# A seven-bank ring of TensorE results laid out as three pairs and a single bank, with the softmax normalisation moved to GpSimd

## The chip, the cores and the metric

The kernel runs on one core of one Trainium2 chip. The metric is the device time of one execution in microseconds, and less is better. Times of an execution are read from the trace of one profiled execution.

## The reference, cut to what matters

The input x is 8 images of 256 channels by 1024 pixels (32x32). Four blocks follow each other:

```python
# L0: single-head self-attention with 32 latent channels over the 1024 pixels, then attention over 128 concepts
# L1: a 10-class map, its norms, a small gated MLP, added back to x
# L2: group norm, then 8-head attention, 32 channels per head, over 1024 x 1024 pixels
qkv = einsum('oc,bct->bot', w_qkv, group_norm(x)) + b_qkv
weight = softmax(einsum('bct,bcs->bts', q * scale, k * scale), axis=-1)
a = einsum('bts,bcs->bct', weight, v)
x = x + (einsum('oc,bct->bot', w_proj, a) + b_proj)
# L3: group norm, then for every pixel an attention of its 8 heads with each other, projected and added to x
```

## The kernel before

Everything is float32. The attention of L0 and L2 is done in "windows". A window `u` is one unit: four heads (L2: half the heads of one image, so two windows an image, `par` 0 and 1) or four images of L0's one head. There are 2 windows of L0 and 16 of L2, 18 in all, each of `STEPS` = 16 steps. A window has two halves of eight steps. A half holds 512 queries, and each of its steps takes 128 keys.

All five engines run through the same list of steps, each with its own instruction order, written out by `window_jobs`. In step s TensorE does, in this order:

- `scores(u, par, s)`, L626 to L638: the scores of four heads, 128 keys by 512 queries each, as four rounds of four matmuls (32 contraction rows a head; HI and LO are a split of the float32 values, and the last round adds the negated maximum). Each head has a PSUM bank of its own.
- `values(u, par, s - 1)`, L652: eight matmul instructions that add exp(scores) x V of the step before into the bank AV. In text, V.
- the jobs of the step, `jobs[s]`. The one in nearly every step is `max`, L603: four matmuls of the scores in the other orientation (128 queries by 512 keys), whose row maxima VectorE takes for a coming half (`row_max`, L1292). The eight of a half stand in its first seven steps, two of them in step 1. Others are `qk` (L688; VectorE splits it at L1267 and L1268), `v` (L678), `post` (the output projection, L705), `sums` (L662 and L667, the softmax sums over the keys; step 1 of each half), `flip` (turns the maxima, last step of each half) and `spread` (L712, step 6 of each half).

ScalarE takes exp of each head's bank (L1034) into the buffer PR, which holds four steps. GpSimd adds the exps of the steps of a half (L1201, twelve adds a half, two a step), beginning once the `sums` of the half before are done (`half_done`), and it may lag some steps behind. In one window of each image GpSimd also makes the next image's normalised input (`norm_apply`, L1172 to L1181).

Every result that TensorE leaves in PSUM for another engine takes the next bank of a ring of seven; the eighth bank is AV. TensorE may write a bank once its last reader has released it. When it wants a bank that isn't free it waits, and so does all that is behind it, since its instructions stay in order. The helpers at issue:

```python
def fill(reader, tally, back):          # TensorE
    slot = ring.place()
    if slot in held:
        wait(pe, *held[slot])
    held[slot] = (reader, tally.now() - back)
    return RING[slot]
```

At the end of a half its unnormalised output must leave AV, and its sums are inverted:

- ScalarE copies AV to OHU after the exps of the next half's step 0 (`keep_values`, L1000). It first waits for `norm_done`, which says that the outputs of the half before that are normalised. The first V of the next half, which TensorE issues in its step 1, waits for this copy (`half_kept`).
- ScalarE copies the sums to RC (`keep_sums`, L1006), and a DMA spreads them over R16. VectorE inverts R16 (`invert`, step 3). A DMA brings the inverses back to RC (`return_inverse`, step 4). TensorE's `spread` multiplies them by a block matrix, which repeats the row of each head over its 32 rows of PSUM (step 6), and VectorE multiplies OHU by it (`normalise`, L1317) and raises `norm_done`.

After the windows comes L3, with other code. It takes about the last quarter of the time.

Of the kernel before, what the change touches and what calls it, by code (L numbers as in the profile page):

```python
# [15 lines left out]

# [9 lines left out]
D = 32  # L26
# [3 lines left out]
EXPS = H * STEPS  # L30
SLOTS = 7
# [5 lines left out]
RETURN_AT = 4  # L37
SPREAD_AT = 6
# [28 lines left out]
class Ring:  # L67


    def __init__(self):  # L70
        self.at, self.slots = 0, tuple(range(SLOTS))

    def place(self):
        self.at += 1
        return self.slots[(self.at - 1) % len(self.slots)]
# [4 lines left out]
    def align(self, to=0):  # L80
        while self.at % SLOTS != to:
            self.at += 1

    def only(self, slot):
        self.at, self.slots = 0, (slot,)


def places(job, single):

    if job[0] == "v":  # L90
        return 2 if single else 1
    return {"max": 4, "stats": 0, "negate": 0, "reread": 0, "concepts": 4, "softmax": 0, "turn": 4,
            "classes": 2, "norms": 2, "pool": 0, "regate": 0, "write": 4}.get(job[0], 1)
# [9 lines left out]
QK_ORDER = ((1, 0), (1, 1), (0, 0), (0, 1))  # L103


def maxima(half):

    return [("max", half, t, keys) for t in range(TILES_HALF) for keys in range(2)]


def window_jobs(post=False, nxt=True, gn=False, ahead=0, trail=True, single=False):
# [5 lines left out]
    for half in range(2):  # L117
# [5 lines left out]
        if half == 1 or trail:  # L123
            jobs[first + SUM_AT].insert(1, ("sums",))
            jobs[first + SPREAD_AT].append(("spread", half - 1))
    if nxt:
        for step, job in zip((1, 2, 3, MT + (3 if post or gn or single else 7)), QK_ORDER):
            jobs[step].append(("qk",) + job)
        parts = (6, MT + 1) if single else (7, MT + 1, MT + 1, MT + 2) if gn else (4, 6, 7, MT + 2)
        for n, step in enumerate(parts):  # L130
            jobs[step].append(("v", n))
    if post:
        for step, job in zip((4, 6, MT + 4, MT + 7), ((0, 0), (1, 0), (0, 1), (1, 1))):
            jobs[step].append(("post",) + job)
    if ahead:
# [3 lines left out]
        jobs[first + 2].append(("gn", 0, ahead))  # L139
    if gn:  # L140
        jobs[MT + 4].append(("gn", 1, 1))
# [29 lines left out]
def first_jobs():  # L171
# [6 lines left out]
            ("norms",): [("v", n) for n in range(4)]}  # L178
# [8 lines left out]
def program(nc, x, w_l0, w_o, w_o_t, concepts, concepts_t, gammas, conv_w, conv_wt, conv_b, lin1_t, lin2_t,  # L187
# [8 lines left out]
    with ctx:  # L196
# [19 lines left out]
        RC = sb("RC", [P, HALF])  # L216

# [116 lines left out]
        RING = [S4[:, n, :] for n in range(4)] + [RB[:, 0, :], RB[:, 1, :], SUM[:, :]]  # L334
        RING_SUM, RING_LAST = 6, 5
# [21 lines left out]
        stage_ready = sem("stage_ready")  # L357
# [10 lines left out]
        inverse_in = sem("inverse_in")  # L368
        norm_done = sem("norm_done")
# [1396 lines left out]
```

## Time and profile before

| | |
|---|---|
| median of 3 runs | 1921.55 us (1916.68 to 1927.38) |
| the profiled execution | 1920.26 us, of which the span of the trace is 1918.5 us |
| busy share of the span | PE (TensorE matmul) 89%, DVE (VectorE) 72%, POOL (GpSimd) 71%, ACT (ScalarE) 41%, PEld (TensorE weight load) 40% |

The busy time of PE is modelled: matmuls overlap each other in the array, and each is drawn with its whole latency. So a stretch with PE at 99% can still hold time in which TensorE issues nothing. That is better seen in the starts of its instructions.

### The profile page before, as it was taken

How to read it: one execution, taken by the hardware profiler on the slowest of the kernel's cores; microseconds unless marked ns; L12 is line 12 of the kernel's file. 1: busy time of each engine (PE TensorE's matmuls, PEld its weight loads, DVE VectorE, ACT ScalarE, POOL GpSimd, SP SyncE). 2: the span in 40 equal slices, each digit the busy share in tenths (PEclk: the TensorE clock that was granted, in tenths of full speed). 3: DMA queues.
4: the chain of work that ended last, by engine and by line, in shares of the span. 5: the costliest groups of instructions: out<-in, count | busy, mean ns of one | idle time of the engine just before them, and what ended most of it. 6: DMA issues, size and time to landing. Idle time of an engine off the chain costs nothing.

```text
span 1918.5 us, 37187 instructions
## 1 busy us (share of the span) xinstructions
PE 1702.5 (89%) x15160; PEld 773.6 (40%) x15160; DVE 1374.5 (72%) x2153; ACT 787.1 (41%) x1546; POOL 1357.7 (71%) x581
## 2 busy tenths in 40 slices
PE   5897765799999999999999999999997678889974
PEld 2332222344344444344344344444442345555541
DVE  5677567887777877767867877777771158878875
ACT  0352401155455555455455455455555233333320
POOL 0573600088788887887888878878789059989996
PEclk8898887799999999999999999999998889999986
DMA  5000030220001001001001010010010211222211
GB/s 189 1 2 1 2 129 0 84 77 23 2 2 67 2 2 67 2 9 60 2 24 45 2 59 11 1 67 2 2 45 1 89 29 55 88 77 75 74 51 47
DMA packets 48432, 75.11 MB, mean 39 GB/s; under 512 B 30804, under 2 KB 31110, under 8 KB 48262
## 3 DMA queue, kind: packets, MB, share of 16 engines
q1 hardware_dynamic: 38758, 72.15, 10.6%
q8 instruction: 120, 1.97, 0.4%
q10 hardware_dynamic: 9504, 0.59, 0.3%
q14 instruction: 50, 0.41, 0.1%
HBM read 44.87 MB, written 25.17 MB: 37 GB/s over the span
## 4 chain that ended last, share of the span: by engine, by line
PE 77%; DVE 13%; issue 3%; ACT 2%; DMA 2%; POOL 1%; SPq 1%; POOLq 0%; DVEq 0%; ACTq 0%
PE AV L652 14%; DVE MX L1292 7%; PE S L626 6%; PE RB L895 6%; PE S L688 4%; PE S L603 3%; PE AV L908 3%; PE RB L626 3%; PE RB L944 3%; PE S L638 2%; PE RB L603 2%; PE S L630 2%; PE S L678 2%; PE RB L688 2%; PE S L634 2%
## 5 line engine op out<-in xcount | busy, mean ns | idle before, releaser
L1201 POOL TENSOR_TENSOR ACC<-ACC,PR 128x1024 f32<-128x1024 f32 x360 | 840.9, 2373 | 34.4 <-ACT PR L1034 34.4
L1034 ACT ACTIVATE PR<-S 128x512 f32<-128x512 f32 x667 | 358.6, 603 | 373.1 <-PE S L638 242.9
L1292 DVE TENSOR_REDUCE MX<-S 128x1 f32<-128x512 f32 x646 | 409.4, 681 | 124.2 <-PE RB L603 60.5
L1201 POOL TENSOR_TENSOR ACC<-PR 128x1024 f32<-128x1024 f32 x72 | 168.9, 2368 | 343.0 <-ACT PR L1034 131.6
L652 PE MATMUL AV<-PR,VT 128*32 128x512 f32 x2304 | 312.9, 616 | 3.8 <-ACT PR L1034 3.3
L1292 DVE TENSOR_REDUCE MX<-RB 128x1 f32<-128x512 f32 x336 | 218.5, 681 | 73.8 <-PE S L603 57.0
L1034 ACT ACTIVATE PR<-RB 128x512 f32<-128x512 f32 x328 | 183.7, 604 | 168.9 <-PE S L638 63.4
L626 PE MATMUL S<-HI 32*128 32x512 f32 x667 | 195.6, 493 | 6.2 <-DVE NMR L1305 2.5
L1227 POOL TENSOR_TENSOR PR<-WO,WRK 128x1792 f32<-128x1792 f32 x32 | 155.6, 4883 | 27.9 <-DMA WO<-WO 12.9
L1227 POOL TENSOR_TENSOR PR<-WO,VT 128x1792 f32<-128x1792 f32 x32 | 155.0, 4867 | 10.3 <-DMA WO<-WO 8.3
L603 PE MATMUL S<-HI 32*128 32x512 f32 x646 | 156.2, 507 | 3.4 <-ACT PR L1034 2.8
L1651 DVE TENSOR_REDUCE ENC<-PR 128x256 f32<-128x2048 f32 x64 | 145.9, 2280 | 15.7 <-issue 7.4
L630 PE MATMUL S<-LO,HI 32*128 32x512 f32 x667 | 143.1, 431 | 0.0
L1292 DVE TENSOR_REDUCE MX<-SUM 128x1 f32<-128x512 f32 x170 | 115.8, 681 | 34.4 <-PE S L603 33.7
L638 PE MATMUL S<-NMR,ONER 32*128 32x512 f32 x667 | 131.6, 397 | 0.0
L634 PE MATMUL S<-HI,LO 32*128 32x512 f32 x667 | 131.2, 397 | 0.0
L1034 ACT ACTIVATE PR<-SUM 128x512 f32<-128x512 f32 x157 | 94.8, 604 | 75.3 <-PE S L638 69.1
L626 PEld LDWEIGHTS S<-HI 32*128 32x128 f32 x667 | 78.7, 183 | 108.9 <-ACT PR L1034 39.2
L626 PE MATMUL RB<-HI 32*128 32x512 f32 x328 | 118.1, 491 | 4.0 <-ACT PR L1034 2.0
L603 PE MATMUL RB<-HI 32*128 32x512 f32 x336 | 111.5, 509 | 11.1 <-DVE MX L1292 11.1
L895 PE MATMUL RB<-X 128*32 128x256 f32 x1792 | 111.7, 390 | 10.6 <-ACT X L1099 4.2
L603 PEld LDWEIGHTS S<-HI 32*128 32x128 f32 x646 | 59.4, 186 | 140.3 <-DVE MX L1292 48.7
(357 smaller groups left out, 3250.9 us busy)
## 6 DMA issues: line engine op xcount, KB each, us to landing
X<-out_y SPq DMA_DIRECT2D x24, 1024.0 KB, 5.0
out_y<-X SPq DMA_DIRECT2D x16, 1024.0 KB, 4.9
X<-in_x SPq DMA_DIRECT2D x8, 1024.0 KB, 8.5
OHU<-out_y SPq DMA_DIRECT2D x8, 512.0 KB, 4.4
X<-out_y SPq DMA_DIRECT2D x8, 512.0 KB, 4.1
out_y<-X SPq DMA_DIRECT2D x8, 512.0 KB, 3.1
out_y<-OHU SPq DMA_DIRECT2D x8, 512.0 KB, 3.1
WO<-WO SPq DMA_DIRECT2D x128, 16.0 KB, 1.9
```

Of the source, the lines that this page charges most:

```text
L603: mm(bank(), HI[par][D * h:D * h + D, 0, first:first + P], HI[par][D * h:D * h + D, 1, HALF * keys:HALF * keys + HALF], start=True, stop=T ...
L626: mm(dst[h], HI[par][row, 1, keys], HI[par][row, 0, cols], start=True, stop=False, skip_group_check=True)
L630: mm(dst[h], HI[par][row, 1, keys], LO[par][row, 0, cols], start=False, stop=False, skip_group_check=True)
L634: mm(dst[h], LO[par][row, 1, keys], HI[par][row, 0, cols], start=False, stop=False, skip_group_check=True)
L638: mm(dst[h], ONER[row, :], NMR[row, half, :], start=False, stop=True, skip_group_check=True).then_inc(st_full, 1)
L652: last = mm(AV[D * h:D * h + D, :], VT[par][:, mt, D * h:D * h + D], exps(s, h // 2)[:, HALF * (h % 2):HALF * (h % 2) + HALF], start=(mt = ...
L895: last = mm(dst[D * j:D * j + D, QUARTER * (h % 2):QUARTER * (h % 2) + QUARTER], W3[:, t, C * which + D * h:C * which + D * h + D], xn3(b) ...
L1034: nc.scalar.activation(exps(s, pair)[:, HALF * one:HALF * one + HALF], RING[ring.place()], ACT.Exp, scale=1.0 if i is None else float(D) * ...
L1201: nc.gpsimd.tensor_tensor(ACC[:, pair, :], so_far, exps(s, pair), ALU.add).then_inc(pool_used, 1)
L1227: nc.gpsimd.tensor_tensor(PV[n % 2].rearrange("p (h d g) -> p h d g", h=NHEAD, d=D)[:, heads], PTK[:, st, heads, j, :].unsqueeze(2).broadc ...
L1292: nc.vector.tensor_reduce(out=MX[:, h, t, keys:keys + 1], in_=bank(), op=ALU.max, axis=AX.X).then_inc(ring_free, 1)
L1651: nc.vector.tensor_reduce(out=O3[n % 2], in_=PV[n % 2].rearrange("p (c g) -> p c g", g=NHEAD), op=ALU.add, axis=AX.X).then_inc(o_ready3, 1)
```

## The change

It does four things.

1. The ring is made of three pairs of banks (`PAIR`, `SLOTS` = 3) in place of seven banks. The four heads' scores take two pairs, and so does a `max`. A pair has one release for both its banks. ScalarE takes exp of a pair in one instruction of 128x1024 in place of two of 128x512, and `row_max` reduces a pair in one instruction. The seventh bank, SUM, is a single one (`Single`) outside the ring. `qk`, `v`, `post`, `gn` and `sums` all use it, one after the other.
2. `spread` on TensorE and `normalise` on VectorE go, in L2's windows, and become `settle`: in step 5 of a half ScalarE issues a DMA that repeats the inverses over the rows (`repeat_inverse`, 128 rows of 512 into the new buffer INV), and GpSimd multiplies OHU by it (128x512) after its adds of step 6. GpSimd's multiply raises `norm_done`. There are 31 of these; L0's and the last half keep `spread`.
3. `v` is done four key tiles at a time: two jobs of 16 matmuls a window in place of four of 8.
4. Jobs move. `qk` goes from steps 1, 2, 3 and 11 or 15 to steps 0, 2, 8 and 10, and the order of its four parts changes. `v` goes to steps 4 and 7 or 3 and 7; `post` goes from 4, 6, 12, 15 to 3, 5, 12, 15; `gn` 1 goes from step 12 to 11 (13 in the first image). The `max` tiles go over the first 512 keys and then the second. The semaphore `stage_ready` is dropped for a wait on `ring_free`.

```diff
-SLOTS = 7
+SLOTS = 3
+REPEAT_AT = 5
...
-            jobs[first + SPREAD_AT].append(("spread", half - 1))
+            jobs[first + SPREAD_AT].append(("settle" if settle else "spread", half - 1))
     if nxt:
-        for step, job in zip((1, 2, 3, MT + (3 if post or gn or single else 7)), QK_ORDER):
+        for step, job in zip((1, 2, 3, MT + 3) if single else (0, 2, MT, MT + 2), QK_ORDER):
             jobs[step].append(("qk",) + job)
-        parts = (6, MT + 1) if single else (7, MT + 1, MT + 1, MT + 2) if gn else (4, 6, 7, MT + 2)
-        for n, step in enumerate(parts):
+        for n, step in enumerate((6, MT + 1) if single else (4, 7) if gn else (3, 7)):
             jobs[step].append(("v", n))
...
-        RING = [S4[:, n, :] for n in range(4)] + [RB[:, 0, :], RB[:, 1, :], SUM[:, :]]
-        RING_SUM, RING_LAST = 6, 5
+        PAIR = [S4[:, 0:2, :], S4[:, 2:4, :], RB[:, 0:2, :]]
+        SINGLE = (SUM[:, :], RB[:, 1, :])
...
+            def pair(reader, count):
 
                 slot = ring.place()
                 if slot in held:
                     wait(pe, *held[slot])
-                held[slot] = (reader, tally.now() - back)
-                return RING[slot]
+                held[slot] = (reader, count)
+                return PAIR[slot]
+
+            def single(reader, count):
+
+                if "single" in held:
+                    wait(pe, *held["single"])
+                held["single"] = (reader, count)
+                return spot.bank()
...
                 for h in range(H):
                     row = slice(D * h, D * h + D)
-                    exped.add()
-                    dst.append(fill(exp_done, exped, 0))
+                    if h % 2 == 0:
+                        two = pair(exp_done, exped.add())
+                    dst.append(two[:, h % 2, :])
...
+            def repeat_inverse(n):
+
+                wait(act, inverse_in, 16 * (n + 1))
+                act.dma_start(INV[:, :],
+                              RC[0:P:D, :].unsqueeze(1).broadcast_to([H, D, HALF])).then_inc(repeat_in, 16)
...
-                        nc.scalar.activation(exps(s, pair)[:, HALF * one:HALF * one + HALF],
-                                             RING[ring.place()], ACT.Exp,
+                        nc.scalar.activation(exps(s, pair),
+                                             PAIR[ring.place()].rearrange("p a q -> p (a q)"), ACT.Exp,
...
+                    if jobs and ("settle", half - 1) in jobs[s]:
+
+                        own, n = par if half else 1 - par, 2 * u + half - 1
+                        wait(pool, repeat_in, 16 * (n - 3))
+                        nc.gpsimd.tensor_tensor(OH[own][1 - half], OH[own][1 - half], INV[:, :],
+                                                ALU.mult).then_inc(norm_done, 1)
...
             def row_max(half, t, keys):
-                for h in range(H):
-                    nc.vector.tensor_reduce(out=MX[:, h, t, keys:keys + 1], in_=bank(), op=ALU.max,
-                                            axis=AX.X).then_inc(ring_free, 1)
+                for pair in range(2):
+                    wait(dve, ring_full, drained.add())
+                    nc.vector.tensor_reduce(out=MX[:, 2 * pair:2 * pair + 2, t, keys], in_=PAIR[ring.place()],
+                                            op=ALU.max, axis=AX.X).then_inc(ring_free, 1)
```

## Rows read from the trace of the kernel before

**Rows 1.** The page: busy time by engine, and the chain's shares.

```profile
PE 1702.5 (89%) x15160; PEld 773.6 (40%) x15160; DVE 1374.5 (72%) x2153; ACT 787.1 (41%) x1546; POOL 1357.7 (71%) x581
...
PE 77%; DVE 13%; issue 3%; ACT 2%; DMA 2%; POOL 1%; SPq 1%; POOLq 0%; DVEq 0%; ACTq 0%
```

**Rows 2.** Timeline of PE in one image: start us, length us, V.

```profile
1005.55 1.07 PE L652 MATMUL AV<-PR,VT 128*32 128x512 f32 x8
...
1016.93 1.06 PE L652 MATMUL AV<-PR,VT 128*32 128x512 f32 x8
...
1021.41 1.06 PE L652 MATMUL AV<-PR,VT 128*32 128x512 f32 x8
...
1040.52 1.06 PE L652 MATMUL AV<-PR,VT 128*32 128x512 f32 x8
...
1046.30 1.06 PE L652 MATMUL AV<-PR,VT 128*32 128x512 f32 x8
```

**Rows 3.** Timeline of all engines in step 0 of a window.

```profile
1002.17 1.06 PE L652 MATMUL AV<-PR,VT 128*32 128x512 f32 x8
1002.27 2.06 ACT L1034 ACTIVATE PR<-S 128x512 f32<-128x512 f32 x4 [2.34 <-PE S L638]
...
1003.16 0.50 PE L603 MATMUL RB<-HI 32*128 32x512 f32 x2
...
1003.70 1.29 DVE L1292 TENSOR_REDUCE MX<-RB 128x1 f32<-128x512 f32 x2 [1.81 <-PE S L603]
...
1004.20 0.63 ACT L1000 ACTIVATE OHU<-AV 128x512 f32<-128x512 f32 x1
...
1004.44 0.49 PE L626 MATMUL RB<-HI 32*128 32x512 f32 x1
```

**Rows 4.** Groups by line on DVE: count, busy us, mean ns of one.

```profile
L1292 DVE TENSOR_REDUCE MX<-S 128x1 f32<-128x512 f32 x646 | 409.4, 681 | 124.2 <-PE RB L603 60.5 <-PE S L603 42.0 <-PE SUM L603 19.9
...
L1610 DVE TENSOR_REDUCE SUM<-S 128x256 f32<-128x2048 f32 x16 | 36.7, 2296 | 0.9 <-PE S L923 0.6
L1268 DVE SCALAR_TENSOR_TENSOR LO<-S,X,HI 128x512 fp32r<-128x512 f32 x36 | 27.0, 751 | 1.3
...
L1317 DVE TENSOR_TENSOR OHU<-OHU,S 128x512 f32<-128x512 f32 x22 | 14.9, 676 | 15.0 <-PE S L712 15.0
```

**Rows 5.** Chain that ended last, in order of time: its jobs on TensorE.

```profile
960.00 1.06 PE S L712 x2
...
974.31 1.09 PE S L678 x8
...
1007.06 1.00 PE S L662 x8
1008.05 0.86 PE S L667 x8
...
1018.43 1.92 PE RB L688 x4
```

**Rows 6.** Timeline of POOL over the two windows of one image.

```profile
938.25 4.70 POOL L1201 TENSOR_TENSOR ACC<-PR 128x1024 f32<-128x1024 f32 x2 [7.01 <-PE S L667]
...
974.05 4.69 POOL L1201 TENSOR_TENSOR ACC<-PR 128x1024 f32<-128x1024 f32 x2 [7.85 <-PE RB L667]
...
996.62 9.39 POOL L1201 TENSOR_TENSOR ACC<-ACC,PR 128x1024 f32<-128x1024 f32 x4
1009.38 4.69 POOL L1201 TENSOR_TENSOR ACC<-PR 128x1024 f32<-128x1024 f32 x2 [3.37 <-PE S L667]
1014.03 23.32 POOL L1201 TENSOR_TENSOR ACC<-ACC,PR 128x1024 f32<-128x1024 f32 x10
1044.06 4.70 POOL L1201 TENSOR_TENSOR ACC<-PR 128x1024 f32<-128x1024 f32 x2 [6.71 <-PE RB L667]
...
1077.50 4.69 POOL L1201 TENSOR_TENSOR ACC<-PR 128x1024 f32<-128x1024 f32 x2 [5.45 <-PE RB L667]
```

**Rows 7.** DMA issues: size, median us from issue to landing.

```profile
OHU<-out_y SPq DMA_DIRECT2D x8, 512.0 KB, 4.4
```

More of the change, by code:

```diff
@@ L70, in __init__, with align, bank, last @@
     def __init__(self):
-        self.at, self.slots = 0, tuple(range(SLOTS))
+        self.at = 0
     def place(self):
         self.at += 1
-        return self.slots[(self.at - 1) % len(self.slots)]
+        return (self.at - 1) % SLOTS
     def skip(self, n):
         self.at += n
-    def align(self, to=0):
-        while self.at % SLOTS != to:
+    def align(self):
+        while self.at % SLOTS:
             self.at += 1
[L84 to L93, printed above, removed]
+class Single:
+    def __init__(self, banks):
+        self.n, self.banks = 0, banks
+    def bank(self):
+        return self.banks[self.n]
+    def last(self):
+        self.n = 1
+def places(job):
+    return {"max": 2, "flip": 1, "settle": 0, "concepts": 2, "turn": 2, "classes": 1, "norms": 1, "write": 2}.get(job[0], 0)
 def wait(eng, sem, value):
@@ L690, in qk_product @@
                 last.then_inc(ring_full, 1)
+                kept_qk[u, which, half] = drained.now()
             def group_sums(k, batch):
@@ L818, in after @@
                         pe.wait_ge(pe_ready, pe_need.add())
-                    dst = [bank() for _ in range(H)]
+                    dst = banks() + banks()
                     for j in range(H):
@@ L1050, in window @@
                         return_inverse(2 * u)
+                    for half in range(2):
+                        if s == MT * half + REPEAT_AT and ("settle", half - 1) in jobs[MT * half + SPREAD_AT]:
+                            repeat_inverse(2 * u + half - 1)
                     if early:
@@ L1253, in link, with bank, banks, split_qk @@
                 dve.wait_ge(dve_step, steps.add())
-            def bank():
+            def bank(wide=False):
                 wait(dve, ring_full, drained.add())
-                return RING[ring.place()]
+                return PAIR[ring.place()][:, 0, :] if wide else spot.bank()
+            def banks():
+                two = PAIR[ring.place()]
+                for part in range(2):
+                    wait(dve, ring_full, drained.add())
+                    yield two[:, part, :]
             def own():
                 dve.wait_ge(ring_free, drained.now())
-            def split_qk(bias, which, half, par):
-                src = bank()
+            def split_qk(bias, which, half, par, wide=False):
+                src = bank(wide)
                 cols = slice(HALF * half, HALF * half + HALF)
@@ L1442, in after @@
                 elif what == "classes":
-                    for part in range(2):
+                    for part, src in enumerate(banks()):
                         cols = slice(HALF * part, HALF * part + HALF)
-                        src = bank()
                         link(nc.vector.tensor_scalar(OM[g][:, cols], src, CB[:, :], None, ALU.add))
@@ L1581, in _ @@
             own()
-            ring.only(RING_LAST)
+            spot.last()
             invert(2 * (2 * B + 1) + 1)
```

195 lines of the change are left out of this document (105 added, 90 removed).

## The prediction, made before the change was run

> **What bounds the kernel now.** I read the page first. TensorE's matmuls are busy for 89% of the span and make 77% of the chain that ended last; VectorE makes 13% of it [rows 1]. That says "TensorE", but a busy PE is drawn with latencies, so I went to the timeline of one image of L2 and took the distance from one V to the next as the length of a step. Most of the change lies in the sixteen windows of L2.
>
> Two kinds of step show two limits. A step with a `qk` job takes 1021.41 - 1016.93 = 4.48 us [rows 2]. It adds up as TensorE's own work with no wait in it: V 1.0, `max` 0.43, `qk` 1.92 [rows 5] and the four rounds of scores 1.13. A step with no job but `max` takes 1005.55 - 1002.17 = 3.38 us [rows 2, 3], though the same sum without `qk` is only 2.5. The missing 0.9 us is a wait for banks, and rows 3 show it: after the `max` matmuls (1003.16) TensorE wants to start the next scores, but the last of their four first-round matmuls (L626) starts only at 1004.44. Two releases come together there. ScalarE's four exps end at 1002.27 + 2.06 = 1004.33. VectorE's first row maximum begins at 1003.70 and takes 0.68, so it ends at 1004.38 [rows 3, 4]. The path through VectorE is, from V's start: V 0.99, matmul and hand-over 0.54, maximum 0.68, hand-over 0.06, then the rest of the scores 1.11. That is 3.38. So a free step is paced by the round trip of a bank, and only a job of about 1 us or more hides it.
>
> The second thing to see is GpSimd. From one half's first add to the next it is 35.8, 35.3, 34.7 and 33.4 us, 139.25 an image [rows 6]. The twelve adds take 4.69 + 23.3 = 28.0, and GpSimd then idles for 7.85, 3.37, 6.71 and 5.45 us until `sums` are done. In the half with 3.37 it also makes the next image's input, 3.9 us: eight adds from 974.05 at 4.69 a pair of adds end at 992.8, and the next begins at 996.62 [rows 6].
>
> **The change part by part.**
>
> *The pairs.* In the ring of seven, the first bank of `max` is released after one head's maximum. In the ring of three pairs the positions run scores, scores, max, max, so the second pair of a step's scores always takes the pair that the first pair of the last `max` had. It is released after a maximum over 128x1024. No row shows that shape. It costs at most two of today's, 1.36, and at least what 1024 of the 2048 columns of L1610 take, 1.15. The line through 512 and 2048 columns (681 and 2296 ns, 1.05 ns a column) gives 1.22, and I take that [rows 4]. A free step becomes 0.99 + 0.54 + 1.22 + 0.06 + 1.11 = 3.92 us, 0.54 longer, with 3.85 to 4.06 as the bounds. Could ScalarE set it? Its two exps of 128x1024 take at most the 2.06 of today's four [rows 3], so they release at 2.2 from V's start, while VectorE releases at 2.8. ScalarE's gain is hidden, and so is VectorE's (two reductions in about 2.4 against four in 2.5).
>
> The step with `sums` has two `max` tiles. Today without a `qk` it takes 1046.30 - 1040.52 = 5.78 [rows 2]. In the new order VectorE starts the first tile's pairs at 1.53 and ends them at 3.9. The second tile's first pair ends at 5.1 (1.22 later; its matmul stands behind the `sums`, 1.0 + 0.86 [rows 5], and is ready by 3.9). Then 0.06 and 1.11 follow: 6.25. The `qk` that used to stand behind it and hide this wait has moved to step 0.
>
> A step with a job on the single bank keeps its length, 4.48 for `qk` and `post`, about 4.5 for a `v` of 16 matmuls (twice 1.09 less what they share [rows 5]). The single bank must be free for the next step's job. VectorE ends its maxima at 3.9 and a `qk`'s split (two of 0.75 [rows 4]) at 5.4, and the next job starts at 4.48 + 1.4, so this holds. If a step's VectorE work were 0.5 longer it would not.
>
> *`spread` and `normalise`.* TensorE loses 1.06 us in each of 31 halves [rows 5], 33 us of work in all. In two of an image's four halves `spread` is the step's only job, where 0.9 of its 1.06 lies in the wait for banks; the step is then a free one again. VectorE loses 0.68 a half [rows 4], which nobody waits for.
>
> *`settle`.* GpSimd gains a multiply of 128x512, half of an add of 2.35, so 1.2 us [rows 6]. The Trainium skill, GPSIMD Engine Reference, section 3.1, has a two-input float32 operation of 2048 columns at 4497 ns on GpSimd and about half on VectorE, so it speaks against this move. By its figure the multiply would be 1.1 and each GpSimd-bound half 0.1 shorter.
>
> The place matters more than the price. `settle` is in step 6 of the list, but GpSimd does it after all twelve adds, which end 28 us after `sums`. ScalarE's `keep_values` at the next half's step 0 waits for `norm_done`. Behind it on ScalarE stand the exps of step 1, and behind its copy stands TensorE's first V. So the half gets a floor that it does not have today, a closed loop: adds 28.0, `settle` 1.2, hand-over 0.1, copy 0.63 [rows 3], hand-over 0.1, and from V's start through `max` and `sums` to GpSimd's first add 3.5 to 3.8 (1040.52 to 1044.06, 1005.55 to 1009.38 [rows 2, 6]), say 3.6. That is 33.6 us a half, and 3.9 more, 37.5, for the half with the input of the next image.
>
> *The repeat DMA.* It moves 256 KB in step 5. A transfer of 512 KB lands in 4.4 us [rows 7]. GpSimd wants it after its last add, at about 1014.03 + 23.3 = 1037.4, and step 5's exps end near 1031, so 6 us of cover hide it. Its issue on ScalarE lies in that engine's idle time. What it costs if late is one for one, in every half. The Trainium skill, DMA: Bandwidth & Descriptors, "Rules for kernel authors", says that a transfer whose outermost dimension is under 16 is confined to that many DMA engines, and here it is 4. That speaks against the change. With the page's 436 GB/s over 16 engines and its 2 us of fixed cost I estimate 4.4 us, still under the cover.
>
> *The jobs' new places.* Free steps rise: an image has 11 now (steps 11, 13, 14 and 6 of its first window, 4, 5, 6, 11 to 14 of its second).
>
> *The sum for an image*, a half from step 1 to the next step 0. Steps with flip and a job are 4.3 (V 1.0, flip 0.3, job 1.9, scores 1.1), with flip alone 3.5.
> - First: 6.25 + 4.48 x4 (2, 3, 5, next 0) + 4.5 + 3.92 + 4.3 = 36.9, against 35.8.
> - Second: 6.25 + 4.48 x3 + 3.92 x3 + 4.3 = 35.75, but GpSimd's floor is 37.5, against 35.3.
> - Third: 6.25 + 4.48 x2 + 4.5 + 3.92 x3 + 4.3 = 35.8, against 34.7.
> - Fourth: 6.25 + 4.48 x2 + 3.92 x4 + 3.5 = 34.4, against 33.4.
>
> That is 144.6 against 139.2, so +5.4 us an image and +43 for eight. In L0's two windows some eight free steps and two with `sums` gain 0.5 each, +5. In the last window, where no `max` fills the steps, both halves show `settle` and the copy behind it, +2. The serial stages of L1 and L3 keep their work. The sum is +50 on 1920.3, the profiled execution. It lies 0.07% under the median, so I use the same number for both: 1971.
>
> **The rivals.**
> 1. *The ring costs nothing and only GpSimd's floor acts.* This would be so if the drain of a pair overlapped more than I think. Free steps at 3.39 and `sums` steps at 5.78 give halves of 35.9, 37.5, 33.7 and (by the floor) 33.6, 140.7 an image: +12 in all, 1932. Against it, today's free step is just as long as its VectorE path.
> 2. *Only the ring costs.* If GpSimd reaches `settle` earlier than I think, the second half is 35.75: 1956. Against it, its adds leave no gaps [rows 6].
> 3. *Faster.* With neither, the halves are 35.9, 33.7, 33.7 and 31.8, 135.1 an image: -33 in all, 1888. It is the removed `spread` work coming through. It needs the floor gone, and a pair released within 0.95 us instead of 1.22 (4.1 us of gain spread over 15 steps that wait is 0.27 each). With the floor it cannot be faster.
> 4. *Worse.* The pair's maximum costs 1.36, two of today's: 15 steps times 0.14 on eight images, +17, 1987. A late repeat DMA would come on top.
>
> **How the numbers follow.** Forecast 0.62, rival 2 0.12, rival 1 0.10, rival 3 0.08, rival 4 0.08. The forecast's own range, from the bounds of the pair's maximum, is 1962 to 1987. The range that holds eight in ten reaches down to rivals 2 and 1 and up to rival 4: 1936 to 1990. A change under 0.5% can't be told from none here. Slower than that: the forecast, rivals 2 and 4, and half of rival 1, 0.87. Within it 0.05. Faster 0.08.
>
> **What would show it.** Free steps of 3.9 us, with the second pair's first-round matmul behind a DVE release. DVE reductions of 1.2 us. `sums` steps of 6.2. In one half of four, ScalarE's copy of AV behind GpSimd's multiply, and halves of 37.5. GpSimd idle before its first add 4 us or less there, less the multiply. I am wrong if the reductions of a pair take well under 1.1, if GpSimd's multiply ends long before the copy wants it, or if a job on the single bank waits for the one before it.

## The result, and the profile after

The changed kernel takes 1982.5 us (median of four runs, 1979.8 to 1986.5), the kernel before 1924.4 beside it on the same chip (four runs, 1916.7 to 1927.4). The ratio is 1.031, with a 95% interval of 1.027 to 1.035: slower by 58 us. The profiled execution of the changed kernel has a span of 1984.5 us, 66.0 more than the 1918.5 before. That is more than the medians differ by, because one profiled execution lies 4 us over its median and the other 4 us under it.

The page of the changed kernel, the lines that answer to [rows 1] and [rows 4], and the new transfer (columns as there):

```profile
PE 1655.7 (83%) x15098; PEld 743.6 (37%) x15098; DVE 1317.8 (66%) x1514; ACT 752.4 (38%) x970; POOL 1394.9 (70%) x612
...
PE 63%; DVE 18%; issue 8%; POOL 6%; ACT 3%; DMA 2%; POOLq 0%; SPq 0%; DVEq 0%; ACTq 0%
...
L1349 DVE TENSOR_REDUCE MX<-S 128x2 f32<-128x1024 f32 x395 | 472.7, 1220 | 222.2 <-PE S L633 182.4
L1079 ACT ACTIVATE PR<-S 128x1024 f32<-128x1024 f32 x396 | 393.3, 1021 | 505.0 <-PE S L671 410.5
...
INV<-RC ACTq DMA_DIRECT2D x31, 256.0 KB
```

TensorE, VectorE and ScalarE all have less to do than before (TensorE 47 us less, VectorE 57, ScalarE 35), and the span is longer. TensorE's share of the last chain fell from 77% to 63%; VectorE, GpSimd and "issue" took what it lost. GpSimd alone has more to do (37 us; its 31 new multiplies of 1.28 take 40). So the time is not lost in work, the engines wait for each other more. Where they wait is seen in the distances from V to V, the steps of the prediction (TensorE's timeline of one half after; answers to [rows 2]; V is L687 now):

```profile
1015.45 1.07 PE L687 MATMUL AV<-PR,VT 128*32 128x512 f32 x8
...
1021.87 1.06 PE L687 MATMUL AV<-PR,VT 128*32 128x512 f32 x8
...
1026.34 1.06 PE L687 MATMUL AV<-PR,VT 128*32 128x512 f32 x8
...
1030.30 1.07 PE L687 MATMUL AV<-PR,VT 128*32 128x512 f32 x8
...
1034.78 1.06 PE L687 MATMUL AV<-PR,VT 128*32 128x512 f32 x8
...
1046.78 1.06 PE L687 MATMUL AV<-PR,VT 128*32 128x512 f32 x8
...
1053.02 1.06 PE L687 MATMUL AV<-PR,VT 128*32 128x512 f32 x8 [1.49 <-ACT OHU L1041]
```

The step with `sums` takes 6.42, the one with a `qk` behind it 4.47, the free one 3.96, and the last step of this half 6.24, where the same kind of step takes 4.65 in the other three halves. A free step from the inside (timeline of all engines; answers to [rows 3]):

```profile
1034.88 1.02 ACT L1079 ACTIVATE PR<-S 128x1024 f32<-128x1024 f32 x1 [2.75 <-PE RB L671]
...
1035.77 0.69 PE L633 MATMUL S<-HI 32*128 32x512 f32 x4
1035.80 1.02 ACT L1079 ACTIVATE PR<-RB 128x1024 f32<-128x1024 f32 x1
1036.32 2.36 DVE L1349 TENSOR_REDUCE MX<-S 128x2 f32<-128x1024 f32 x2 [1.47 <-PE S L633]
...
1036.88 0.50 PE L659 MATMUL RB<-HI 32*128 32x512 f32 x2 [0.41 <-ACT PR L1079]
...
1037.60 0.50 PE L659 MATMUL S<-HI 32*128 32x512 f32 x2 [0.22 <-DVE MX L1349]
```

ScalarE's second exp ends at 1036.82 and lets the first pair of new scores start at 1036.88. The second pair stands until 1037.60, and the bracket names VectorE's maximum: the first of two began at 1036.32 and takes 1.22, so it ends at 1037.54. From V's start at 1034.78 it is 1.54 to the maximum, 1.22 for it, 0.06, and 1.13 to the next V: 3.95.

The end of the second half, with `settle` in it (timeline of all engines):

```profile
1051.00 1.28 POOL L1253 TENSOR_TENSOR OHU<-OHU,INV 128x512 f32<-128x512 f32 x1
...
1052.37 0.60 ACT L1041 ACTIVATE OHU<-AV 128x512 f32<-128x512 f32 x1 [3.53 <-POOL OHU L1253]
1052.86 1.02 ACT L1079 ACTIVATE PR<-S 128x1024 f32<-128x1024 f32 x1
...
1053.02 1.06 PE L687 MATMUL AV<-PR,VT 128*32 128x512 f32 x8 [1.49 <-ACT OHU L1041]
```

ScalarE idles for 3.53 us until GpSimd's multiply is done, TensorE's V waits for ScalarE's copy, and the exps of the step stand behind the copy, though their scores are ready at 1051.5. The halves, from one first add of GpSimd to the next (its timeline over one image; answers to [rows 6]):

```profile
1019.17 4.69 POOL L1247 TENSOR_TENSOR ACC<-PR 128x1024 f32<-128x1024 f32 x2 [8.53 <-PE SUM L701]
...
1037.07 13.97 POOL L1247 TENSOR_TENSOR ACC<-ACC,PR 128x1024 f32<-128x1024 f32 x6
...
1056.55 4.69 POOL L1247 TENSOR_TENSOR ACC<-PR 128x1024 f32<-128x1024 f32 x2 [4.28 <-PE SUM L701]
...
1092.81 4.69 POOL L1247 TENSOR_TENSOR ACC<-PR 128x1024 f32<-128x1024 f32 x2 [7.07 <-PE SUM L701]
...
1127.40 4.69 POOL L1247 TENSOR_TENSOR ACC<-PR 128x1024 f32<-128x1024 f32 x2 [5.41 <-PE SUM L701]
```

The half before these (from 981.46) took 37.7 us, then come 37.4, 36.3 and 34.6: 145.9 an image, against 139.25 before. The image of [rows 6] is a quick one of the kernel before: in four of its first seven images the fourth half takes 35.0 instead of 33.4, and the seven take 140.0 on average (the reason stands with experiment 8). Six adds, 13.97 us, begin at 1037.07 without a gap, and `settle` follows them at 1051.00.

### The profile page after: what moved, and what is told of

It is laid out like the page before. It is cut to its first block, busy times and chain, and to the rows that moved or that the text cites. A ratio compares the mean times of both kernels' runs of the same rounds, so it can differ in the third digit from the quotient of the medians.

```text
span 1984.5 us, 35745 instructions
## 1 busy us (share of the span) xinstructions
PE 1655.7 (83%) x15098; PEld 743.6 (37%) x15098; DVE 1317.8 (66%) x1514; ACT 752.4 (38%) x970; POOL 1394.9 (70%) x612
## 4 chain that ended last, share of the span: by engine, by line
PE 63%; DVE 18%; issue 8%; POOL 6%; ACT 3%; DMA 2%; POOLq 0%; SPq 0%; DVEq 0%; ACTq 0%
PE AV L687 12%; DVE MX L1349 11%; PE RB L936 6%; PE SUM L722 5%; PE S L633 4%; POOL ACC L1247 3%; PE S L659 3%; PE AV L949 3%; PE SUM L712 3%; PE RB L985 2%; PE RB L659 2%; PE S L671 2%; PE RB L633 2%; PE S L663 2%; PE S L667 2%
## 5 line engine op out<-in xcount | busy, mean ns | idle before, releaser
L1247 POOL TENSOR_TENSOR ACC<-ACC,PR 128x1024 f32<-128x1024 f32 x360 | 840.2, 2377 | 34.4 <-ACT PR L1079 34.3
L1349 DVE TENSOR_REDUCE MX<-S 128x2 f32<-128x1024 f32 x395 | 472.7, 1220 | 222.2 <-PE S L633 182.4
L1079 ACT ACTIVATE PR<-S 128x1024 f32<-128x1024 f32 x396 | 393.3, 1021 | 505.0 <-PE S L671 410.5
L687 PE MATMUL AV<-PR,VT 128*32 128x512 f32 x2304 | 311.2, 612 | 16.5 <-ACT OHU L1041 12.9
L1349 DVE TENSOR_REDUCE MX<-RB 128x2 f32<-128x1024 f32 x181 | 220.7, 1219 | 106.6 <-PE RB L633 94.3
L1079 ACT ACTIVATE PR<-RB 128x1024 f32<-128x1024 f32 x180 | 183.9, 1022 | 174.3 <-PE RB L671 93.6
L659 PE MATMUL S<-HI 32*128 32x512 f32 x792 | 171.9, 501 | 66.8 <-DVE MX L1349 28.9
L633 PE MATMUL S<-HI 32*128 32x512 f32 x790 | 158.7, 512 | 11.4 <-DVE MX L1349 6.8
L1708 DVE TENSOR_REDUCE ENC<-PR 128x256 f32<-128x2048 f32 x64 | 145.9, 2280 | 14.7 <-issue 7.0
L663 PE MATMUL S<-LO,HI 32*128 32x512 f32 x792 | 138.7, 423 | 0.0
L659 PEld LDWEIGHTS S<-HI 32*128 32x128 f32 x792 | 64.1, 183 | 180.0 <-DVE MX L1349 63.9
L659 PE MATMUL RB<-HI 32*128 32x512 f32 x360 | 90.9, 501 | 41.4 <-DVE MX L1349 31.9
L633 PEld LDWEIGHTS S<-HI 32*128 32x128 f32 x790 | 63.4, 187 | 165.0 <-issue 94.8
L722 PE MATMUL SUM<-X 128*128 128x512 f32 x240 | 121.1, 628 | 0.0
L633 PE MATMUL RB<-HI 32*128 32x512 f32 x362 | 92.9, 509 | 13.6 <-DVE MX L1349 12.1
L1218 POOL TENSOR_TENSOR RSTD<-VE,MHALF 128x2 f32<-128x2 f32 x16 | 11.2, 703 | 121.1 <-DVEq L1405 121.1
```

The source lines that it names most:

```text
L633: last = mm(dst[:, h % 2, :], HI[par][D * h:D * h + D, 0, first:first + P], HI[par][D * h:D * h + D, 1, HALF * keys:HALF * keys + HALF], s ...
L659: mm(dst[h], HI[par][row, 1, keys], HI[par][row, 0, cols], start=True, stop=False, skip_group_check=True)
L663: mm(dst[h], HI[par][row, 1, keys], LO[par][row, 0, cols], start=False, stop=False, skip_group_check=True)
L687: last = mm(AV[D * h:D * h + D, :], VT[par][:, mt, D * h:D * h + D], exps(s, h // 2)[:, HALF * (h % 2):HALF * (h % 2) + HALF], start=(mt = ...
L722: last = mm(dst, WQK[:, t, unit, which, :], XN[:, t, HALF * half:HALF * half + HALF], start=(t == 0), stop=(t == CT - 1))
L1079: nc.scalar.activation(exps(s, pair), PAIR[ring.place()].rearrange("p a q -> p (a q)"), ACT.Exp, scale=1.0 if i is None else float(D) ** - ...
```

## The experiments

Eleven kernels were run. The times are medians of 4 to 8 runs, and each ratio is to the kernel before on the same chip (1920.5 to 1922.0 us). Kernels that ran on different chips are compared through these, so differences of a few us between them are not firm. Four start from the changed kernel and take a single suspect away; four start from the kernel before and add a part of the change without the pairs; three try what the others pointed to.

**1. The floor taken away.** The copy of the values waits for all multiplies so far. It overwrites a buffer other than the one that the last `settle` works on, so it can wait for one fewer.

```diff
-                wait(act, norm_done, 2 * u + half)
+                wait(act, norm_done, 2 * u + half - (1 if u > 2 else 0))
```

> The changed kernel, but ScalarE's copy of AV (keep_values) waits for one normalised half fewer, so GpSimd's multiply no longer stands before it. The buffers it protects are ordered by other waits. My theory: three costs lie in the changed kernel, the drain of a pair (free steps 3.94, sums steps 6.41), the floor through GpSimd in one half of four (37.4), and, not foreseen, a wait of 0.17 us of the second max pair for the exp of the first scores pair in steps with a job (4.65 instead of 4.48). This run takes away the floor alone: the half of 37.4 falls to about 36.4, the other three stay, some 8 us less in all, about 1975. Rival 'only the ring costs': nothing moves, 1982. Rival 'the floor is most of it': 1940 or less.

Measured: 1972.1 us, ratio 1.027 (1.025 to 1.029). The second half fell from 37.4 to 36.0 and the others stayed (37.7, 36.3, 34.6). The floor is real and costs 1.4 us an image, 10 us in all by the medians (8 by the two ratios). Rival 2, that only the ring costs, is out, and so is rival 1: with the floor gone 51 us are left.

**2. `spread` and `normalise` put back**, in the ring of pairs, on TensorE and VectorE, with no `settle` and no repeat DMA.

```diff
-            window(u, 0, window_jobs(post=not first, gn=True, ahead=int(first), trail=not first,
-                                      settle=True), i)
+            window(u, 0, window_jobs(post=not first, gn=True, ahead=int(first), trail=not first), i)
-            window(u + 1, 1, window_jobs(nxt=not last, ahead=0 if last else 2, settle=True), i)
+            window(u + 1, 1, window_jobs(nxt=not last, ahead=0 if last else 2), i)
```

> The changed kernel with the normalisation put back: the inverse sums repeated by TensorE's spread in steps 6 and 14, multiplied by VectorE, no repeat DMA, no multiply on GpSimd. The ring of pairs stays. My theory: the two spreads of a window stand in free steps, where 1.06 us of TensorE work fits in the wait for the pair, so they cost nothing, and the floor is gone as in e1: about 1975. Rival 'the removed TensorE work is a real gain': 31 times 1.06 us come back, 2007.

Measured: 1968.3 us, 1.025 (1.023 to 1.027). The halves are those of experiment 1 (37.7, 36.0, 36.3, 34.6; the second is 36.3 in two images), though TensorE has 24 us more busy time (1673.7 against 1649.6). In a ring of pairs the 1.06 us of `spread` lie wholly in the wait for the pair. What the change removes from TensorE brings it nothing there.

**3. The maximum over half the columns**, so that a pair is released sooner.

```diff
-    ..., t, keys], in_=PAIR[ring.place()],
+    ..., t, keys], in_=PAIR[ring.place()][:, :, 0:HALF // 2],
```

> The changed kernel, but each row maximum reads only the first 256 keys of each of its two banks (it leaves out half of the keys from the maximum that is subtracted before exp), so a pair is drained in about 0.68 us instead of 1.22. Same matmuls, same ring. My theory: free steps fall from 3.94 to about 3.4, where ScalarE's exps pace them, sums steps from 6.41 to 5.7; the second half stays at its floor 37.4 and the fourth stops at 33.6: about 5 us an image, 1943. Rival 'the pair's drain is hidden': less than 5 us in all.

Measured: 1940.8 us, 1.009 (1.006 to 1.012). VectorE's groups by line (columns as in [rows 4]):

```profile
L1349 DVE TENSOR_REDUCE MX<-S 128x2 f32<-128x512 f32 x395 | 262.0, 687 | 322.1 <-PE S L633 268.0 <-PE RB L633 53.6
```

The maximum went from 1.22 to 0.69, and with it the free step from 3.94 to 3.41 and the `sums` step from 6.42 to 5.88: both by the 0.53 that was taken off. A job step kept its 4.65. So the free steps are paced by VectorE's release, one for one.

The total, 2 us from what I expected, is a hit by luck and says little of the free steps. In the profiled executions this kernel is 42 us shorter than the changed one, and 26 of them lie ahead of GpSimd's first add of L2 (at 364.86 instead of 390.68), earlier than even the kernel before has it (377.29), since the maxima are short in L0 and in the stages of L1 too. The halves of a middle image are 36.6, 39.0 to 40.3, 34.2 and 33.5, so an image gains 1 to 3 us where I had 5: the wait at the floor grew to 3.7 us of idle time before V, the granted clock was 0.57 in the 4 us after it (1012 to 1016 us), and the `sums` step there took 7.33.

**4. The exps of L2 over half the columns.** The other half of PR keeps old values, so the output is wrong and only the time is read.

```diff
-    nc.scalar.activation(exps(s, pair),
-                         PAIR[ring.place()].rearrange("p a q -> p (a q)"), ACT.Exp,
+    nc.scalar.activation(exps(s, pair).rearrange("p (a q) -> p a q", a=2)[:, :, 0:cut],
+                         PAIR[ring.place()][:, :, 0:cut], ACT.Exp,
```

> The changed kernel, but in L2's windows each exp treats only the first 256 queries of each of its two banks (the rest of PR keeps old values), so it takes about 0.6 us instead of 1.02. My theory: free steps stay at 3.94, since VectorE's drain paces them; steps with a job fall from 4.65 to 4.48, since the second max pair no longer waits for the exp of the first scores pair; with one half of four at its floor that is about 13 us, 1970. Rival 'ScalarE paces the free steps': they fall by 0.4 and more, and the time by 35 us.

Measured: 1974.5 us, 1.027 (1.025 to 1.029). Free steps stayed at 3.94, so ScalarE doesn't pace them. But a job step behind another job step fell from 4.65 to 4.49, and the `sums` step from 6.42 to 6.23. There is a second wait, then, of 0.17 us. The total is 4 us over what I expected, because the second half is 39.0 instead of 37.4 in four of the six middle images, with a granted clock of 0.63 behind the wait at the floor (1044 to 1048 us). It can be seen in a job step of the changed kernel (timeline of all engines, V at 988.64):

```profile
988.75 1.02 ACT L1079 ACTIVATE PR<-RB 128x1024 f32<-128x1024 f32 x1 [2.75 <-PE RB L671]
...
989.63 0.50 PE L633 MATMUL S<-HI 32*128 32x512 f32 x2
...
989.83 0.50 PE L633 MATMUL RB<-HI 32*128 32x512 f32 x2
```

The second pair of `max` matmuls takes the pair that the step's first scores had. That exp begins after V does, because here both pairs of scores ran side by side and were ready late, and ends at 989.77. The matmul follows at 989.83, where the banks that are free let all four start together (L633 x4 above). In the ring of seven the first `max` bank was one that had long been read.

**5. `settle` alone, on the kernel before**: seven banks, the old places of the jobs, the repeat DMA and the multiply on GpSimd.

```diff
+INV = sb("INV", [P, HALF])
+act.dma_start(INV[:, :], RC[0:P:D, :].unsqueeze(1).broadcast_to([H, D, HALF])).then_inc(repeat_in, 16)
+nc.gpsimd.tensor_tensor(OH[own][1 - half], OH[own][1 - half], INV[:, :], ALU.mult).then_inc(norm_done, 1)
-            jobs[first + SPREAD_AT].append(("spread", half - 1))
+            jobs[first + SPREAD_AT].append(("settle" if settle else "spread", half - 1))
```

> The kernel before, with its ring of seven banks and its order of jobs, and only the normalisation changed: repeat DMA and multiply on GpSimd (settle), with the wait of the copy of AV as it is. My theory: each half loses up to the 1.06 us of spread on TensorE (34.7, then 33.7 and 32.8 for the third and fourth), but the half that also makes the next image's input rises from 35.3 to its floor of 37.4, and the fourth stops at about 33.6. Sum about 139.4 against 139.25: no change, 1920 to 1930. Rival 'TensorE's work bounds': 33 us less, 1890.

Measured: 1950.4 us, 1.015 (1.012 to 1.018). I had expected a gain or no change. The halves are 34.95, 40.3, 33.85 and 34.3, against 35.8, 35.3, 34.7 and 33.4. Three of the four are near or under the old ones, and the floor's half is 5 us over. The floor in TensorE's timeline, and under it in ScalarE's:

```profile
1158.38 1.06 PE L655 MATMUL AV<-PR,VT 128*32 128x512 f32 x8
...
1164.82 1.94 PE L655 MATMUL AV<-PR,VT 128*32 128x512 f32 x8 [2.98 <-ACT OHU L1003]
...
1174.47 1.07 PE L655 MATMUL AV<-PR,VT 128*32 128x512 f32 x8
```

```profile
1164.17 0.60 ACT L1003 ACTIVATE OHU<-AV 128x512 f32<-128x512 f32 x1 [3.64 <-POOL OHU L1219]
```

The floor step takes 6.44 instead of 3.39, which the closed loop gives. The next step takes 9.65 instead of 6.77, which it does not give. V itself takes 1.94 instead of 1.06 in it. The windows of 4 us tell why (busy time of each engine, then PEclk, the granted clock):

```profile
1156.00:1160.00 4.00, 4.00 (x33) 1.47 (x31) 1.17 (x3) 1.75 (x5) 4.00 (x2) 1.00 0.23 92
1160.00:1164.00 4.00, 1.84 (x16) 1.00 (x15) 2.39 (x4) 0.53 (x2) 4.00 (x3) 1.00 0.44 172
1164.00:1168.00 4.00, 3.18 (x16) 0.70 (x20) 0.49 (x1) 2.55 (x5) 0.08 (x1) 0.52 0.90 306
1168.00:1172.00 4.00, 4.00 (x22) 0.93 (x15) 2.47 (x5) 0.60 (x1) 0.77 (x1) 0.63 0.53 218
```

TensorE was busy for 1.84 of the 4 us at the floor, then the granted clock fell to 0.52 over the next 4, about the lower of its two levels (1.2 GHz), and was back at 1.00 from 1172 us on. The wait cost 3.05 us, the clock behind it 2.9 more.

**6. The same with the relaxed wait of experiment 1.**

> As b1_settle, but the copy of AV waits for one normalised half fewer. My theory: the floor is gone and the removed spread comes through where it stood beside another job (two halves by 1.06, two by 0.6): 3.3 us an image, 26 in all, about 1897, faster than both kernels. Rival 'settle on GpSimd is no gain at all': 1924.

Measured: 1908.1 us, 0.995 (0.993 to 0.996). The undisturbed halves are 34.95, 34.4, 33.9 and 32.8, 136.05 an image, as worked out. The total is 11 us over the expectation, because the wait isn't relaxed in the first window of the first image, whose second half took 40.6, and some fourth halves took 34.3 to 37.9.

**7. The jobs' new places alone, on the kernel before** (seven banks, `spread` kept).

```diff
-QK_ORDER = ((1, 0), (1, 1), (0, 0), (0, 1))
+QK_ORDER = ((1, 0), (0, 0), (1, 1), (0, 1))
-        for step, job in zip((1, 2, 3, MT + (3 if post or gn or single else 7)), QK_ORDER):
+        for step, job in zip((1, 2, 3, MT + 3) if single else (0, 2, MT, MT + 2), QK_ORDER):
-        for step, job in zip((4, 6, MT + 4, MT + 7), ((0, 0), (1, 0), (0, 1), (1, 1))):
+        for step, job in zip((3, 5, MT + 4, MT + 7), ((0, 0), (1, 0), (0, 1), (1, 1))):
```

> The kernel before, with its ring of seven banks and its normalisation, and only the jobs moved as in the change (qk in steps 0, 2, 8, 10, v as two jobs of 16 matmuls, post, gn, order of the maxima). My theory: the loss of the change is none of this. The qk in step 0 fills a free step, and sums no longer stand beside it: halves of about 36.5, 34.3, 34.3 and 32.3, 137.4 an image, 1909 in all. Rival 'the new order of the jobs is what costs': slower than 1924, up to 1960.

Measured: 1932.1 us, 1.006 (1.004 to 1.008), 12 us slower than the kernel before, where I had expected a gain of 12. Undisturbed halves are 36.55, 34.8, 34.35 and 34.19, 139.9 an image against 139.2. The first and third are as worked out, the second is 0.5 over and the fourth 1.9. My sum had put nothing for `stats` and `gn`, the statistics of the next image's input, which VectorE and TensorE make in step 11 of the first window and steps 12 and 13 of the second.

**8. Settle, relaxed wait and new places together, still on seven banks.**

> The kernel before with its ring of seven banks, and all else of the change (moved jobs, settle on GpSimd), the copy of AV waiting for one normalised half fewer. My theory: everything but the ring of pairs is a gain when the floor is gone; b3's 137.4 loses 0.6 for each spread in a nearly free step: about 135 an image, 1890. Rival 'the parts cancel': 1910 to 1925.

Measured: 1924.4 us, 1.002 (1.001 to 1.004). That is 34 us over what I expected. Undisturbed halves are 35.9, 34.1, 33.7 and 33.5, 137.2 an image, 1.1 over experiment 6. This kernel differs from experiment 1 in the ring alone (pairs, and the single bank for the jobs), and the two are 48 us apart.

Two things that I had left out show here. In the ring of seven the `gn` step 11 takes 4.01 and steps 12 and 13 take 4.06 and 4.65, where a free step takes 3.39, 2.5 us an image; in the ring of pairs the same three take 3.94 to 3.96, so the wait for the pair hides them. And in four of the six middle images the fourth half takes 35.9 to 36.3 instead of 33.5, because the granted clock falls behind step 13. The kernel before has this too (4-us windows, columns as in experiment 5; its step 13 there began at 1196.70 and took 5.52 instead of 4.66):

```profile
1192.00:1196.00 4.00, 3.57 (x36) 1.43 (x32) 3.93 (x9) 2.06 (x4) 4.00 (x3) 1.00 0.01 2
1196.00:1200.00 4.00, 3.25 (x30) 1.31 (x22) 3.82 (x8) 2.06 (x4) 4.00 (x3) 1.00 0.02 2
1200.00:1204.00 4.00, 3.90 (x26) 1.44 (x25) 1.92 (x8) 2.06 (x4) 4.00 (x3) 0.57 0.00 0
```

In the changed kernel the granted clock is 1.00 in every such window of the middle images. So the ring of pairs costs more than its total shows: 7.4 us in an undisturbed image (144.6 in experiment 1 against 137.2), from which 2.4 to 2.7 go off for each fall of the clock that doesn't happen. In the profiled executions the two kernels are 48 us apart, 34 of them in the six middle images and 10 ahead of L2's first add.

**9. V between the two pairs of `max`**, on the changed kernel: the first pair's matmuls stand ahead of V, and VectorE starts on them 0.7 us after the last round of scores begins, where the changed kernel needs 1.87.

```diff
+                    if early:
+                        part(0)
                     if s:
                         values(u, par, s - 1)
...
+                    if early:
+                        part(1)
```

> The changed kernel with V issued between the two max pairs of a step instead of before both; everything else as it is. My theory: the first max pair is then filled a V (1.0 us) earlier, so its drain of 1.22 us ends before the next scores want the pair, and the second max pair comes when the exp of the first scores pair is done. Free steps fall from 3.94 to the pace of ScalarE, about 3.3, sums steps from 6.41 to 5.9, steps with a job stay near 4.65. The floor through GpSimd stays: halves of 36.6, 37.2, 34.0 and 33.5, about 1945. If TensorE's granted clock falls at places where free steps follow each other, as it did with the short maxima, some 1 to 3 us an image come back. Rival 'the pair ring cannot do better than 3.9 a free step': 1982.

Measured: 1975.1 us, 1.026 (1.023 to 1.029). Free steps fell to 3.25, as expected, and yet the median is 30 us over what I expected and only 7 under the changed kernel. The six runs spread from 1962 to 1993 us, so even the 7 are not firm; the slowest has the lowest mean clock (0.923), the fastest the highest (0.939). The steps got shorter by up to 0.7, GpSimd's loop didn't, so the wait at the floor grew: the floor step is 7.1 to 7.5 us. In three of the six middle images the clock falls behind it in the way of experiment 5 (second half 40.2, third 37.85); in two it does not, with 2.3 us of idle time before V instead of 2.8 (38.55 and 34.7). The falls are those of a wait at the floor, not of free steps that follow each other, as I had guessed from experiment 3.

**10. The same with the relaxed wait**, this time from one half earlier on.

```diff
-                wait(act, norm_done, 2 * u + half)
+                wait(act, norm_done, 2 * u + half - (1 if 2 * u + half > 4 else 0))
```

> As c1_between, and ScalarE's copy of AV waits for one normalised half fewer in all of L2. My theory: without drain stall and floor the changed kernel gets what spread's removal is worth: halves of 36.6, 33.7, 34.0 and 31.7, 136 an image, 1903; with a lower granted clock in places 1905 to 1920. Rival 'two stalls that only hide each other': 1940 and more.

Measured: 1935.8 us, 1.007 (1.005 to 1.009). Halves are 37.6, 34.6, 34.7 and 33.3, 140.2 an image where I expected 136. The step with `sums` was mis-sized and is 3 us of the difference: it takes 6.66, not 5.9 (timeline of its middle):

```profile
1083.93 1.07 PE L687 MATMUL AV<-PR,VT 128*32 128x512 f32 x8
...
1086.24 1.04 PE L701 MATMUL SUM<-ACC,ONES 128*32 128x512 f32 x8
...
1087.21 0.50 PE L633 MATMUL RB<-HI 32*128 32x512 f32 x2
...
1087.75 1.23 DVE L1358 TENSOR_REDUCE MX<-RB 128x2 f32<-128x1024 f32 x1 [1.05 <-PE S L633]
...
1090.58 1.06 PE L687 MATMUL AV<-PR,VT 128*32 128x512 f32 x8
```

VectorE idles for 1.05 us here: the second tile's `max` stands behind both `sums` on TensorE, so the sooner start of the first tile is lost, and the next V now has a `max` pair in front of it (2.83 from the maximum's start to V, 2.41 in the changed kernel). The floor doesn't act.

**11. The kernel before with `settle` on GpSimd and the wait of experiment 10**: no pairs, no moved jobs.

> As b2_settle_relax (seven-bank ring, old order of jobs, settle on GpSimd, relaxed wait), with the wait relaxed in the first image of L2 too, where b2's second half was 40.6. My theory: that half falls to about 35: 5 us less than b2, 1903.

Measured: 1897.2 us (1893.9 to 1900.2), 0.988 (0.986 to 0.990), 6 us under what I expected. This one beats both kernels. It differs from experiment 6 in the wait of one copy, in the first window of L2: the second half there took 34.75 instead of 40.6. GpSimd's timeline in it:

```profile
992.77 1.31 POOL L1219 TENSOR_TENSOR OHU<-OHU,INV 128x512 f32<-128x512 f32 x1
995.23 4.68 POOL L1213 TENSOR_TENSOR ACC<-PR 128x1024 f32<-128x1024 f32 x2 [1.15 <-PE SUM L670]
...
1029.18 4.70 POOL L1213 TENSOR_TENSOR ACC<-PR 128x1024 f32<-128x1024 f32 x2 [4.73 <-PE S L670]
```

In the half with the input of the next image GpSimd ends `settle` at 994.08 and still idles for 1.15 us before the next adds: the multiply fits, once nobody waits for it too soon.

## Why the prediction was right, and where it was off

I forecast 1971 us and slower; it is 1982.5, inside the range, for the two reasons given. The parts of the change, one added to the other, by medians: `settle` with the wait of experiment 1, -12 us (experiment 6 less 1920.5, the kernel before beside it); the new places of the jobs, +16 (experiment 8 less 6, which have the same wait); the pairs, +48 (experiment 1 less 8); the wait of the copy, +10 (the changed kernel less 1). The shares depend on the order. With `spread` kept, the new places cost 12 (experiment 7) and the pairs 36 (experiment 2 less 7): the pairs also swallow the 12 us that `settle` gains without them. And `settle` gains 25 when the wait is relaxed one half earlier (experiment 11).

**Part of the hit is luck.** Two of the prediction's three terms for an image were right. The pairs were to cost 7.8 us (the halves of rival 2, 142.9, against rival 3's 135.1) and cost 7.4; the floor was to cost 1.8 and costs 1.4. But the image with neither, 135.1, is 137.2 (experiment 8), and rival 3's total of 1888, reckoned from it, came out as 1924. Some 10 of these 36 us lie in the one copy whose wait stays as it was in experiment 8 (compare 11 with 6). Of the gain of 33 us that the forecast had counted against the cost of the pairs and the floor, experiment 8 shows nothing. The forecast did not show it, because the ring of pairs hides the `stats` and `gn` steps that the sum had left out, and because it is also free of the falling clock.

**The free step** was 3.92 and is 3.95, and the maximum over a pair 1.22 and is 1.220: the line through the two neighbouring shapes held. Experiment 3 shows that the step follows that one duration. Rival 4, with 1.36, comes near the time (1987), but its cause isn't there.

**"ScalarE's gain is hidden"** is the step that failed, for job steps. I had sized its releases for the next scores alone, and the second `max` pair, too, waits for an exp. That makes a job step behind another one 4.65 instead of 4.48 and is 0.17 of the `sums` step too, 6.42 where I had 6.25. Experiment 4 shows it. The `v` step of 16 matmuls was 4.73, not 4.5. Together this is +0.8 in the first half, +0.5 in the third and +0.2 in the fourth: 145.9 an image, where I had 144.6.

**The floor** was 37.5 and is 37.4. The multiply takes 1.28 where I had 1.2. An estimate from the figure of the Trainium skill (GPSIMD Engine Reference, section 3.1) made it 1.1, so the measurement decides against it by 0.2, which has no weight here. Where `settle` stands in the queue, and who waits for it, mattered more than its price.

**The repeat DMA** never ended a wait. It is issued at 1035.00 in the half shown, and `settle`, 16 us later, begins as the last add ends. Whether its rows being confined to few DMA engines made it slow (the Trainium skill, DMA: Bandwidth & Descriptors, "Rules for kernel authors") the profile doesn't show, since it has no landing time for it.

**`spread`**: the prediction put 0.9 of its 1.06 in the wait for banks. In the ring of pairs it is all of it (experiment 2). In the ring of seven it is 0.4: the step with `spread` alone takes 4.00 in the kernel before and 3.40 in experiment 6, and taking `spread` out is worth 3.2 us an image (136.05 against 139.25, experiments 6 and 11). The saved work is real, and the longer round trip of a pair swallows it.

**Outside the middle images.** L0 cost what was forecast: GpSimd's first add in L0's last half is at 202.84 instead of 197.60, +5 (+7 against experiments 5 and 6, whose L0 is that of the kernel before, at 195.6 and 195.5). What I had at nothing, the serial stages of L1, cost 9 more. These are GpSimd's timelines from the end of L0, the kernel before first, then the changed one:

```profile
301.49 0.71 POOL L1172 TENSOR_TENSOR RSTD<-VE,MHALF 128x2 f32<-128x2 f32 x1 [65.47 <-DVEq L1348]
...
377.29 4.66 POOL L1201 TENSOR_TENSOR ACC<-PR 128x1024 f32<-128x1024 f32 x2 [71.79 <-ACT PR L1034]
```

```profile
305.60 0.71 POOL L1218 TENSOR_TENSOR RSTD<-VE,MHALF 128x2 f32<-128x2 f32 x1 [64.47 <-DVEq L1405]
...
390.68 4.65 POOL L1247 TENSOR_TENSOR ACC<-PR 128x1024 f32<-128x1024 f32 x2 [81.08 <-ACT PR L1079]
```

75.8 us became 85.1. Their work is the same, but the first window's maxima and scores are made in them, through the same ring. With the new places on seven banks (experiments 7 and 8) the distance is 4.7 over that of the kernel before, with the short maximum (experiment 3) 1.7 over it. The first image then took 152.7 us against 141.1, with a granted clock of 0.83 in 380 to 420 us, where the kernel before had 1.00. Why the clock stays low just there was not tried. The last window has the loop of GpSimd in one half, where I had both, at 34.6 against 29.3 us, over twice what I had for the window (31.2 with the relaxed wait of experiment 1); from the first add of the last half on, the changed kernel is 3.6 us faster. In the profiled executions the sum is 5.2 for L0, 9.3 for the serial stages, 56.2 for the 31 halves of the images, less 1.1 between L0 and the first stage and 3.6 at the end: 66.0.

**The new places** cost 1.1 us an image on seven banks. No run takes the jobs one by one, but the steps of experiments 6 and 8 add up to it. The eight small jobs of `v` lengthen their steps by 3.7 us an image together, and their four successors with 16 matmuls by 4.2: the two small ones beside the `flip` of step 7 had been nearly free (3.30 against 3.24 for `flip` alone). `gn` adds 0.1 beside `post` in step 12 and 0.6 by itself in step 11. The `qk` jobs add 0.2 more than they did (0.98 in the `sums` step, 0.88 beside `flip`, 1.1 elsewhere, where all its jobs are now).

**The single bank** that the jobs share never made TensorE wait in the middle images, as the prediction had it: its waits there are for the pairs, for the copy of AV and for the negated maxima.

**What stays open**: why the granted clock falls behind step 13 in some images of a kernel and not in others, and why it stays low at the start of L2.

## What to carry to other kernels

The ring of this kernel is paced by the time from filling to release of one buffer, not by the total work of its readers. Pairing banks makes fewer and cheaper instructions (one maximum of 1.22 us for two of 0.68), and every release later; the steps without other work to cover it lose the difference, here 0.54 us each. Work taken from the engine that looks like the bound is worth only what the steps in which it lies do not spend waiting, so find out first how long that step is with the work and without. A forecast that adds a cost to a better kernel than the one at hand needs a run of that better kernel too: here the sum of the costs was right and what they were added to was not.

When a small operation moves to an engine with a long queue, look for the waits that count it. The multiply cost 1.3 us of an idle engine, and a gain (25 us at most) came only when the copy no longer waited for a buffer that it does not touch.

## What the runs showed of the hardware

- A wait of TensorE can cost twice. With 2.98 us of idle time before V (experiment 5) the granted clock fell from 1.00 to 0.52 in the next 4 us and the step after it took 9.65 instead of 6.77. The changed kernel's own wait at the floor, 1.49 us, was followed by a `sums` step of 6.23, no longer than the others. So a kernel with less work on TensorE but one longer wait an image was slower by 30 us than the one it came from. The length of the wait does not decide it alone: in experiment 8 and in the kernel before, step 13 of the second window, with TensorE busy for 3.13 and 3.25 of 4 us, was followed by a granted clock of 0.52 and 0.57 in some images and by 1.00 in others.
- A maximum over two banks of 512 columns takes VectorE 1.22 us against 0.68 for one, and an exp over two takes ScalarE 1.02 against 0.60. The fixed part that pairing saves is 0.14 on the one and 0.18 on the other.
